# Gate and up products of a feed-forward layer by seven-product Strassen, and half of the normalised rows turned inside the recurrence

## What is computed

```python
mod = (_silu(L0_c) @ L0_wmod).reshape(L0_c.shape[0], 6, 1, -1)
...
h = _layernorm(x, axis=-1) * (1 + ca) + sa
x = x + ga * _L0_attn_ref(h, ...)
h = _layernorm(x, axis=-1) * (1 + cb) + sb
x = x + gb * _L0_ffn_ref(h, ...)

def _L0_ffn_ref(x, w_gate, w_up, w_down):
    gate = jnp.einsum('bsd,hd->bsh', x, w_gate)
    up = jnp.einsum('bsd,hd->bsh', x, w_up)
    gated = jax.nn.silu(gate) * up
    return jnp.einsum('bsh,dh->bsd', gated, w_down)
```

## Time and profile before

| | |
|---|---|
| median of 3 runs | 1065.68 us (1064.44 to 1066.08) |
| profiled execution, device time | 1067.39 us |
| its span in the trace | 1065.6 us |
| TensorE / VectorE / ScalarE / GpSimd busy | 96 / 58 / 35 / 21% of the span |
| mean granted TensorE clock | 0.987 |

### The profile page before, as it was taken

How to read it: one execution, slowest core, us unless ns; L and a number is a source line. 1 busy time by engine, 2 the same in 40 slices (tenths; PEclk the granted TensorE clock), 3 DMA queues, 4 the chain that set the end, 5 groups by cost and what they waited for, 6 DMA issues and landing times.

```text
span 1065.6 us, 20179 instructions
## 1 busy us (share of the span) xinstructions
PE 1025.3 (96%) x8112; PEld 822.7 (77%) x8112; DVE 622.8 (58%) x997; ACT 376.1 (35%) x685; POOL 225.6 (21%) x178
## 2 busy tenths in 40 slices
PE   6999999999998999999899999999999999999998
PEld 3776777777677888877777887888888888888886
DVE  6977377899955777878664333243333434334366
ACT  3676684445545343333453112121212212112110
POOL 1312530021025554554301000000000000004191
PEclk8999999999998999999999998999999999999999
DMA  6605236839166566775520001010000101002223
GB/s 216 194 10 158 53 81 188 236 90 227 53 169 137 136 135 145 185 180 138 172 71 29 1 1 60 1 60 1 30 30 1 60 1 48 11 1 70 80 80 118
DMA packets 153437, 97.42 MB, mean 91 GB/s; under 512 B 93568, under 2 KB 130688, under 8 KB 153216
## 3 DMA queue, kind: packets, MB, share of 16 engines
q1 hardware_dynamic: 153344, 96.12, 33.0%
HBM read 64.64 MB, written 31.46 MB: 90 GB/s over the span
## 4 chain that ended last, share of the span: by engine, by line
PE 75%; DVE 10%; ACT 4%; issue 4%; SPq 3%; DMA 3%; POOL 0%; DVEq 0%; ACTq 0%
PE ps L1303 72%; ACT t L1666 3%; DVE t L1937 3%; PE ps L1311 2%; DVE t L2047 2%; SPq L1180 1%; PE ps L1540 1%; DVE t L1942 1%; DVE t L2147 1%; DVE t L1947 1%; DMA scrA<-t 1%; DVE t L2035 1%; DVE t L2168 1%; SPq L1240 1%; DVE t L2158 1%
## 5 line engine op out<-in xcount | busy, mean ns | idle before, releaser
L1303 PE MATMUL ps<-t,t 128*128 128x512 f32 (+6 forms) x7292 | 972.3, 326 | 26.2 <-DVE t L1937 6.1
L1303 PEld LDWEIGHTS ps<-t,t 128*128 128x128 f32 (+4 forms) x7292 | 770.5, 160 | 212.1 <-issue 43.2
L1937 DVE TENSOR_TENSOR t<-ps,t 128x512 f32<-128x512 f32 (+2 forms) x288 | 197.9, 709 | 256.0 <-PE ps L1303 242.0
L1666 ACT ACTIVATE t<-t 128x512 fp32r<-128x512 f32 (+10 forms) x339 | 189.5, 580 | 307.6 <-DVE t L1937 210.5
L1937 DVE TENSOR_TENSOR t<-t,t 128x512 fp32r<-128x512 f32 (+14 forms) x210 | 166.6, 798 | 112.4 <-ACT t L1666 105.6
L1666 ACT ACTIVATE t<-ps 128x512 f32<-128x512 f32 (+5 forms) x202 | 109.4, 553 | 305.4 <-PE ps L1303 288.7
L2428 POOL TENSOR_TENSOR t<-t,t 128x512 f32<-128x512 f32 x16 | 23.0, 1437 | 376.8 <-DVE t L1937 374.7
L2047 DVE SCALAR_TENSOR_TENSOR t<-ps,t,t 128x511 f32<-128x511 f32 (+2 forms) x108 | 80.3, 747 | 3.6 <-ACT t L1666 0.7
L1666 ACT ACTIVATE t<-ps,t 128x512 f32<-128x512 f32 (+2 forms) x93 | 54.7, 619 | 28.1 <-PE ps L1311 11.4
L1311 PE MATMUL ps<-t,t 128*128 128x128 f32 (+1 forms) x340 | 51.9, 283 | 9.6 <-DVE t L1937 6.4
L1311 PEld LDWEIGHTS ps<-t,t 128*128 128x128 f32 (+1 forms) x340 | 37.8, 145 | 19.9 <-DVE t L1937 10.3
(11 more groups left out here) (52 smaller groups left out, 257.3 us busy)
## 6 DMA issues: line engine op xcount, KB each, us to landing
scrU<-t SPq DMA_DIRECT2D x60, 256.0 KB, 2.9
t<-in_wf SPq DMA_DIRECT2D x16, 768.0 KB, 4.4
t<-scrU SPq DMA_DIRECT2D x32, 288.0 KB, 4.8
t<-scrU SPq DMA_DIRECT2D x32, 192.0 KB, 3.6
t<-in_W SPq DMA_DIRECT2D x19, 256.0 KB, 3.0
t<-in_x SPq DMA_DIRECT2D x16, 256.0 KB, 4.0
t<-in_wmod SPq DMA_DIRECT2D x4, 1024.0 KB, 5.6
t<-in_x SPq DMA_DIRECT2D x32, 128.0 KB, 2.9
```

The lines of the kernel that those rows point to most:

```text
L1303: return e.matmul(o, l, r_, start=start, stop=stop, skip_group_check=True)
L1666: return e.activation(o, i, f, **kw)
L1937: return e.tensor_tensor(o, a, b, op)
```

## The change

**The products.** Take the four blocks of a factor (hidden pair times half of the 512 inputs) and of the rows (half of the inputs times one of two sequences). One level of Strassen's scheme in Winograd's form makes the 2x2 block product out of seven products in place of eight. An iteration `it` now covers one pair of hidden blocks for two sequences: seven products for gate, seven for up, each of 2 x 3 = 6 matmuls of 128x512, and eight down products of 6 as before. There are 16 iterations, eight for sequences 0 and 1 and eight for 2 and 3.

**What it adds.** GpSimd makes the sums of the weight blocks (`w_comb`, four operations of 256 columns) and the low parts (`w_low_ff`, one of 1792 columns), for gate and for up, and twice over, since the weights are loaded for each pair of sequences. ScalarE writes the high parts (1792 columns). For the rows GpSimd and VectorE make the sums once per pair of sequences (`t_raw`, `t4`), and seven splits of 1024 columns (`split_h`) take the place of eight of 512. Of the four output tiles of gate and of up, three need two results added: ScalarE copies a partial sum from PSUM while TensorE goes on accumulating in the same bank (`copy_s`), VectorE adds the copy to another bank (`cadd`). In gate and up the third product (P6 of the scheme) waits for the first copy, the fifth (P7) for the second, the sixth (P4) for the third, and the seventh (P3) for the second `cadd`.

**What it moves.** Units 0, 1, 4, 5, 8, 9 of sequences 0 and 1 are turned in slots 3, 4, 7, 8, 11, 12 of the recurrence; ScalarE scales and shifts them, eight operations of 64 columns. Sequences 2 and 3 are turned in iterations 1 and 2. Their rows for the second pass are split at the end of iteration 7. The output of the first pass is finished and stored in iteration 8 (`post_0`), that of the second at the end.

```diff
@@ slot_of, step order of a slot
+        if u in (3, 4, 7, 8, 11, 12):
+            turn_unit(u - 3)
+        if u == 15:
+            turn_unit(13)
         if has_post:
             ringed("po_wo", u - 1, ("v_yg", u))
@@ the seven products: (name, PSUM bank), which weight and which row block each reads
-    def products(q, b):
-        for jj in range(2):
-            j, n = 2 * q + jj, gu["n"]
...
+    GU = [(1, 0), (2, 1), (6, 0), (5, 2), (7, 0), (4, 0), (3, 2)]
+    A_OF = {1: 1, 2: 2, 6: 5, 5: 4, 7: 0, 4: 3, 3: 6}
+    B_OF = {1: 0, 2: 1, 6: 2, 5: 3, 7: 4, 4: 5, 3: 6}
...
+    def iteration(it):
+        n, last = 2 * it, it == 15
+        if it:
+            prod(n, 0)
+            prod(n, 1)
+            copy_s(n, 0)
+            flush()
+            prod(n, 2)
+            cadd(n, 0)
+            prod(n, 3)
+            copy_s(n, 1)
+            step("silu", it=it, t=0)
+            w_high(up_m(it), [("prod", 7 * (n - 1) + 7)])
+            prod(n, 4)
+            down(it - 1, 0)
+            copy_s(n, 2)
+            cadd(n, 1)
...
+        prod(n, 2)
+        cadd(n, 0)
+        step("gated", it=it, t=0)
+        step("fh", it=it, t=0)
+        prod(n, 3)
+        copy_s(n, 1)
...
+        prod(n, 4)
+        if it and not last:
+            down(it - 1, 7)
+        copy_s(n, 2)
+        cadd(n, 1)
+        step("gated", it=it, t=1)
+        w_high_d(it)
...
+        if it == 7:
+            split_h(1, 4, [("prod", 7 * n + 5)])
+            split_h(1, 5, [("prod", 7 * n + 6)], "p")
+            split_h(1, 6, [("prod", 7 * n + 7)])
...
@@ tensor
+            elif kind == "prod":
...
+                elif o == 6:
+                    e.wait_ge(sem("v_c"), 3 * n + 2)
+                else:
+                    e.wait_ge(sem("a_sp"), 3 * n + {2: 1, 4: 2, 5: 3}[o])
@@ gpsimd
+                signal(e.tensor_tensor(r_[:, 4, :], r_[:, 0, :], r_[:, 3, :], ALU.add), "p_ws")
...
+                signal(e.tensor_tensor(WGl[m % 3][:, :, :], WR[st["slot"]][:, :, :], WGh[m % 3][:, :, :].bitcast(f32),
+                                       ALU.subtract), "p_wl")
```

936 lines of the change are left out of this document (545 added, 391 removed).

## The result

The changed kernel takes 1113.05 us (median of 4 runs, 1112.22 to 1113.89) against 1065.88 for the kernel before (1064.44 to 1069.42): ratio 1.0439, 95% interval 1.0407 to 1.0471. It is 47 us slower; the forecast was 21 us slower, and its range ended at 1106. The direction was right and the size was not. The profiled execution has a span of 1110.4 us; the same sum in the prediction came to 1087.3.

The account below looks back on a forecast made before the run. TensorE's slots plus its waits were taken to bound the kernel. 566.0 + 457.7 + 7.4 + 5 + 22 + 12 + 3 + 14.2 gave a 1087.3 us span, median 1087 us, 2% slower; range 1070 to 1104, eight in ten 1052 to 1106.

Parts of the forecast that it names:

- What is removed: Gate and up products: 1344 matmuls in place of 1536, 192 slots fewer on TensorE, 43.3 us saved.
- Recurrence, six slots: Six recurrence slots that turn tiles: the turn and ScalarE's reads cost 1.5 us a slot, 9 us (3 to 13).
- Transition and iteration 0: Start of the feed-forward: third up product stands 7.8 us behind ScalarE's queue; iteration 1 starts at 566 us.
- Waits in every iteration: Feed-forward: 1.45 us an iteration, including 0.37 each in gate and up behind the down product's sum; 22 us altogether.
- FH's chain: Up block: the fifth product waits for the copy behind ScalarE's first FH step, 0.37 us an iteration.
- GpSimd's share of the gated tile: Up block: VectorE's gated tile waits for the rest of a GpSimd weight sum, about 0.35 us on average.
- Ring waits: Down products and turned tiles share two banks: eight waits of 0.6 us, 5 us.
- Between the passes: Seven splits in iteration 7 delay copies: some 10 us, then 2 us in iteration 8; 12 us (5 to 16).
- Clock: After the stands of 7.8 and 6 us the granted clock drops: some 1.5 us lost after each, 3 us (0 to 6).
- Tail: End of the kernel: GpSimd's 16 last operations put the end 14.2 us behind TensorE's slots, 9.6 more than before.
- C: Up blocks: GpSimd's 4.0 us operations block VectorE, fifth product 2 us later in each of 14 iterations; 1115 us, chance 0.07.
- Rival A: Feed-forward: two products cover each copy and cadd, so the waits shrink; 1061 us, or 1055 with reads covered; chance 0.25.

Follow-up runs that it names:

- e12_locks_apart: All edits together, mended to keep VectorE's two-input operations and GpSimd's long ones apart, with further start reordering: 1054.45 us, 0.9886 of the kernel before.
- e9_reads_vector: Changed kernel with the eight scale-and-shift reads of each tile turned in the recurrence on VectorE, not ScalarE: 1106.64 us, ratio 1.0373.
- e5_high_later: Changed kernel with the high part of the second weight set one recurrence slot later on ScalarE: 1107.86 us, ratio 1.0394.
- e3_load_first: Changed kernel with SyncE issuing the next gate weights' load ahead of the last two units' stores: 1107.49 us, ratio 1.0364.
- e6_splits_behind: Changed kernel with the first second-pass split behind iteration 7's first up-block copy, the last three in iteration 8 behind its first copy: 1105.15 us, ratio 1.0374.
- e7: Changed kernel with the last two first-pass output rows behind GpSimd's low part of the down weights in iteration 8: 1111.59 us, ratio 1.0435.
- e10: Changed kernel with first-pass rows 4 to 7 finished later, and each second-pass sum waiting only for its own row's store: 1106.52 us, ratio 1.0385.
- e13_filled_stands: Changed kernel with unused matmuls added to keep TensorE at work in its three long stands: 1109.77 us, ratio 1.0408.
- e4_copy_first: Changed kernel with the copy for iteration 0's third up product ahead of ScalarE's SiLUs and high weights: 1110.32 us, ratio 1.0403.
- e11_all: Changed kernel with all the single reordering edits together, and some more: 1068.41 us, ratio 1.0017.
- e1: Changed kernel with ScalarE's second copy of each up block ahead of its first FH step: 1102.94 us, ratio 1.0330.
- e2: Changed kernel with VectorE's second cadd in gate and up blocks ahead of the down product's sum: 1105.91 us, ratio 1.0348.

## Why the forecast was wrong in size

Three steps failed. The recurrence term left out the weight steps in slots 12 to 14, which cost 7 us. The transition term took the next load for free of SyncE's queue, which cost 7.0. And the clock term counted two stands for 3 us, where five cost 9 to 10. Step by step, as the prediction has them:

- **What is removed** held. 192 slots are gone, and where TensorE is undisturbed a product of six is 1.360 us (1.354 in the sum). The time of e12_locks_apart is the first that is under the kernel before.
- **Recurrence, six slots**, 9 us: the six turn slots cost 6.4 (1.07 each, not 1.5), the mechanism as argued (e9_reads_vector), a little smaller. **The step that failed is what it leaves out**: the weight steps that the change puts into slots 12 to 14. I costed the turns there and not the high part of set 1, which waits on ScalarE for GpSimd and cost 6.3 us (e5_high_later), nor the low part of a set, beside which slot 12 took 0.8 more. The stretch lost 12.6, since it began 0.9 earlier than before.
- **Transition and iteration 0**, iteration 1 at 566: it was 580. I had the right stand (third up product, ScalarE, the copy behind SiLUs and gate weights), at 7.8 for 11.5 us. **The second step that failed** is that I took GpSimd's weight sums to follow its own queue and never put SyncE's queue in the chain. The load is planned behind the last stores, and with it ahead of them the third up product comes 7.0 us sooner; the stand that is then left, 6.93, is the one I had forecast (e3_load_first). A further part is clock, 3.7 us (below). And part is a `cadd` that waits for the last output product because its tile shares memory with the recurrence; it held `t4` and the splits behind it, and TensorE stood 3.34 us. That last was taken out only together with other edits, so its own price was not measured.
- **Waits in every iteration**, 22 us: right by cause. FH's chain has some 0.3 for 0.37 and GpSimd's share of the gated tile 0.34 for 0.35; the sums of the down product have 0.5 for 0.74, and some 0.4 I did not foresee. That the sum is so near (1.56 for 1.45) is luck in so far as the last two cancel. **Ring waits** held: a turned tile and its product are 2.44 us apart, which is 0.6 more than 1.36 for the product and 0.5 for the turn.
- **Between the passes**, 12 us: the windows of iterations 7, 8 and 9 exceed a usual one by 12.7, 3.9 and 2.3 us, 18.9 together, of which 3.7 are the clock's. The copy behind splits was there as forecast (5.84 for 6 to 7; e6_splits_behind). What failed is the 2 us for iteration 8, where I saw VectorE's two operations and not GpSimd's queue: sums that wait for a load, the low part behind them, the stores behind those (e7, e10). The raw sums of iteration 4, costed at nothing, took 0.8 us net (33.0 and 30.5 us for two iterations of 31.36).
- **Clock**, 3 us: the price was near and **the count of stands failed**. I counted 1.5 us for each of two stands, and behind those two 1.3 and 1.4 were lost. The stand of 5.32 us, which I had not in the sum, cost 2.3 (e13_filled_stands; the 1.4 is from there too). By rows of other executions with the same work at full clock, the changed kernel's trace has 2.4 more at 549.64 (24 matmuls in 8.39 us, 6.01 in e13_filled_stands), 1.3 at 569.55 (12 in 4.33, 3.01 in e4_copy_first) and up to 2.3 at the end (60 in 17.56, 15.30 in e12_locks_apart): with the 3.7, about 9 to 10 us.
- **Tail**, 14.2 behind the slots: 15.1, so near in size, but by another way. GpSimd's 16 operations did not end it alone. They stretched VectorE's differences (four in 5.73 us), on which TensorE stood 4.5.
- **The range.** By the rule that the prediction states (the bounds taken by half) the upper end of the forecast comes to 1098 and not 1104. The result lies beyond either.

Of the rivals, C comes nearest by its number (1115), and not by its cause: it wanted the fifth up product 2 us later in each of 14 iterations, and these took 31.36 us. Its mechanism is real, though: it came up in iteration 0, at 0.34 us in most iterations, and in e11_all at longer operations. The Trainium skill ("SBUF — State Buffer", section "Terms", on the shared port pair) says of such a pair that the loser "fully blocks". The rows agree: 4.36 us beside 3.96, and the stretched operation ends 0.55 us after GpSimd's. Rival A (the cover holds, 1055 to 1061) was wrong for this order of the queues and right for another: with the order mended the same arithmetic takes 1054.

The forecast failed where I costed a step on the engine that carries it and not on the queue that it waits for. For the weight steps and for the load, the order of the changed queues, which I had, showed what each waits for.

## What to carry to other kernels

A change that trades the bounding engine's work for work on others pays only after each new step has been followed through every queue that it stands in, DMA issue included; ask of each wait what is queued behind it. Here the order and place of steps alone, with no change in what is computed, are the difference between 4.4% slower and 1.1% faster. A stand that goes may uncover the next (e4, e7), so test two waits that lie one behind the other together. And two gains may hold the same wait (e1 and e2), so do not add them. And on dense schedules keep GpSimd's long operations away from VectorE's with two SBUF inputs.
